# A fused cross-attention and quantised feed-forward kernel: the weights and late inputs are loaded and prepared later

## What is computed

```python
qk = einsum('bhdq,bhdl->bhql', qh, kh) * scale
ret = einsum('bhql,bhdl->bhdq', softmax(qk), vh)      # values = keys = ctx
x = x + gamma * ret
# bit_linear: einsum(activation_quant(x), weight_quant(w))
h = silu(bit_linear(xn, w_gate)) * bit_linear(xn, w_up)   # xn = layernorm(x); w: 1024 x 256
x = x + bit_linear(rms_norm(h, ln_weight), w_down)        # w_down: 256 x 1024
```

## Time and profile before

| | us |
|---|---|
| median of 3 runs | 229.3 |
| the profiled execution, its own time | 227.79 |
| its span in the trace | 226.0 |
| busy in the span: PE / VectorE / ScalarE / GpSimd | 169.6 / 148.8 / 135.3 / 115.8 |

### The profile page before, as it was taken

One profiled execution on the slowest core, in us unless ns is written; L12 is line 12 of the kernel. 1 busy time (PEld: TensorE's weight loads), 2 busy tenths in 40 slices (PEclk: granted clock), 3 DMA queues, 4 the chain that ended last, 5 costly groups with the idle time before them and its releaser, 6 DMA issues.

```text
span 226.0 us, 4319 instructions
## 1 busy us (share of the span) xinstructions
PE 169.6 (75%) x1382; PEld 97.5 (43%) x1382; DVE 148.8 (66%) x284; ACT 135.3 (60%) x274; POOL 115.8 (51%) x290
## 2 busy tenths in 40 slices
PE   0005561787798969898998989889989988973792
PEld 0002530553375533555465556455655644522332
DVE  2304662536465964897997899799899895246283
ACT  3124252653337754868868886886876975971432
POOL 4327435330523173676786587587367448347150
PEclk9999985558569985999999999999999997997589
DMA  5765989318502162026306315422600000000000
GB/s 160 235 135 156 325 214 244 97 20 179 117 0 74 48 151 64 23 70 144 98 17 174 84 40 128 99 83 79 149 11 5 0 28 7 0 23 0 26 0 23
DMA packets 15707, 19.95 MB, mean 88 GB/s; under 512 B 2597, under 2 KB 14005, under 8 KB 14677
## 3 DMA queue, kind: packets, MB, share of 16 engines
q1 hardware_dynamic: 11397, 14.43, 25.6%
q10 hardware_dynamic: 4288, 5.24, 8.3%
HBM read 15.20 MB, written 4.19 MB: 86 GB/s over the span
## 4 chain that ended last, share of the span: by engine, by line
PE 34%; POOL 25%; DVE 12%; issue 11%; DMA 9%; ACT 6%; ACTq 2%; POOLq 0%; DVEq 0%
PE psO L465 7%; PE psA L435 6%; PE psB L449 5%; POOL hw L317 5%; DMA q_stack<-mt 3%; PE psG L538 3%; POOL hq L1020 3%; DMA k_stack<-k_scratch 3%; DVE h L855 2%; DVE mneg L763 2%; DVE gu L844 2%; ACT th L679 2%; PE psG L501 2%; PE psU L501 2%; PE psG L575 2%
## 5 line engine op out<-in xcount | busy, mean ns | idle before, releaser
L763 DVE TENSOR_REDUCE mneg<-psA 128x2 f32<-128x512 f32 x128 | 82.2, 678 | 26.8 <-PE psA L435 26.6
L608 ACT ACTIVATE probs<-psB 128x512 f32<-128x512 f32 x128 | 73.5, 596 | 26.2 <-PE psB L449 25.4
L435 PE MATMUL psA<-k_stack,q_stack 72*128 72x256 bf16 x256 | 53.8, 299 | 19.7 <-DMA k_stack<-k_scratch 19.3
L449 PE MATMUL psB<-q_stack,k_stack 75*128 75x256 bf16 x256 | 51.9, 288 | 6.6 <-DMA q_stack<-mt 4.6
L465 PE MATMUL psO<-probs,vt 128*32 128x256 f32 x512 | 37.7, 416 | 1.0 <-ACT probs L608 1.0
L435 PEld LDWEIGHTS psA<-k_stack,q_stack 72*128 72x128 bf16 x256 | 23.1, 105 | 34.7 <-issue 27.9
L449 PEld LDWEIGHTS psB<-q_stack,k_stack 75*128 75x128 bf16 x256 | 23.5, 102 | 20.9 <-DMA q_stack<-mt 5.4
L317 POOL TENSOR_TENSOR hw<-h,lnw 128x512 f32<-128x512 f32 x15 | 19.2, 1278 | 22.3 <-DVE h L855 13.3
L465 PEld LDWEIGHTS psO<-probs,vt 128*32 128x32 f32 x512 | 14.1, 115 | 15.2 <-issue 8.8
L844 DVE SCALAR_TENSOR_TENSOR gu<-th,psG 128x512 f32<-128x512 f32 x15 | 10.3, 688 | 9.9 <-ACT th L679 9.9
L679 ACT ACTIVATE th<-psG,tscale 128x512 f32<-128x512 f32 x15 | 10.3, 688 | 8.5 <-PE psG L538 8.5
(11 more groups left out here) (134 smaller groups left out, 256.3 us busy)
## 6 DMA issues: line engine op xcount, KB each, us to landing
k_stack<-k_scratch SPq DMA_DIRECT2D x21, 192.0 KB
q_stack<-q_scratch SPq DMA_DIRECT2D x21, 192.0 KB
q_scratch<-q_parts SPq DMA_DIRECT2D x24, 64.0 KB, 2.6
k_scratch<-k_parts SPq DMA_DIRECT2D x21, 64.0 KB, 2.1
w_sb<-in_L_ffn_w_gate_dram ACTq DMA_DIRECT2D x1, 1024.0 KB, 6.0
w_sb<-in_L_ffn_w_up_dram ACTq DMA_DIRECT2D x1, 1024.0 KB, 6.0
w_sb<-in_L_ffn_w_down_dram ACTq DMA_DIRECT2D x1, 1024.0 KB, 15.6
out_dram<-y_sb SPq DMA_DIRECT2D x8, 128.0 KB, 1.9
```

Source lines behind the costliest of these rows:

```text
L435: mm = pe.matmul(psA[n % A_BANKS][:, qt * L:(qt + 1) * L], q_stack[0:STACK, t % NBUF, bh, qt * P:(qt + 1) * P], k_stack[0:STACK, t % NBUF, ...
L449: mm = pe.matmul(psB[b % 2][:, lt * L:(lt + 1) * L], k_stack[:, t % NBUF, bh, lt * P:(lt + 1) * P], q_stack[:, t % NBUF, bh, :], start=Tru ...
L608: act.activation(probs[:, b % RING, :], psB[b % 2][:, :], ACT.Exp, scale=SCALE).then_inc(s_exp, 1)
L763: dve.tensor_reduce(mneg[:, k % MBUF, QT * (bh % HALF):QT * (bh % HALF + 1)], psA[n % A_BANKS][:, :].rearrange("p (q l) -> p q l", q=QT), ...
```

## The change

The gate's load leaves the start of ScalarE's queue, up and down leave its step -4, and the late inputs leave its step 19. All are now issued by SyncE behind a transfer of maxima: tile 3's inputs and the gate behind the second (steps 36, 37), tile 4's inputs and up and down behind the third (52, 53), the inputs of tiles 5 to 7 at step 85. The stack load of tile 1 moves from step 5 to step 21, behind the first transfer of maxima and, within step 21, behind the stores of tile 2, which stand at that step already. The preparation of the gate moves from steps -8 to 17 to steps 38 to 56, that of up from 22 to 40 to 66 to 81, that of down from 34 to 52 to 78 to 97. Six instead of four groups are copied by VectorE. The variances of tiles 3 to 7 are taken in three lots. Waits in the feed-forward part are refined to the weights that are needed.

```diff
-ACT_W, ACT_LATE = -4, 19
-EARLY = 3
+EARLY, FIRST_LOAD = 3, 21
+BULK_W = {37: (0,), 53: (1, 2)}
+BULK_XC = {36: (3, 4), 52: (4, 5), 85: (5, 8)}
...
-ACT_WS, PE_W, DVE_W, POOL_WQ, DVE_WQ = (-8, 22, 34), (3, 26, 38), (3, 26, 38), (4, 27, 39), (8, 32, 44)
-WB = {10: 0, 12: 1, 14: 2, 17: 3, 34: 4, 36: 5, 38: 6, 40: 7, 46: 8, 48: 9, 50: 10, 52: 11}
-WB_ON_DVE = (5, 7, 9, 11)
-POOL_INIT, DVE_STATS = 46, 45
+ACT_WS, PE_W, DVE_W, POOL_WQ, DVE_WQ = (38, 66, 78), (42, 69, 84), (42, 69, 84), (43, 70, 88), (48, 75, 92)
+WB = {50: 0, 52: 1, 54: 2, 56: 3, 76: 4, 78: 5, 80: 6, 81: 7, 94: 8, 95: 9, 96: 10, 97: 11}
+WB_ON_DVE = (1, 3, 5, 7, 9, 11)
+STATS = {-32: (1, 3), 45: (3, 4), 77: (4, 5), 109: (5, 8)}
...
+        def load_xc(eng, a, b):
+            for t in range(a, b):
+                eng.dma_start(x_sb[:, t, :], x_rows[t]).then_inc(s_x[t], DMA)
+                eng.dma_start(c_sb[:, t, :], ctx_rows[t]).then_inc(s_c[t], DMA)
...
+                if m in BULK_W:
+                    for k in BULK_W[m]:
+                        load_w(sp, k)
+                if m in BULK_XC:
+                    load_xc(sp, *BULK_XC[m])
                 t = tile_at(m, SP_STORE)
...
-                t = tile_at(m, SP_LOAD)
+                t = 1 if m == FIRST_LOAD else tile_at(m, SP_LOAD) if m > FIRST_LOAD else None
...
-                            pe.wait_ge(s_wT, 12 - len(WB_ON_DVE))
-                            pe.wait_ge(s_wTd, len(WB_ON_DVE))
+                            for k in (6, 7):
+                                pe.wait_ge(*w_copied(k))
...
-            load_w(act, 0)
...
-                if m == ACT_W:
-                    act.wait_ge(s_first, 2 * PARTS * DMA)
-                    act.wait_ge(s_stack[0], 2 * PARTS * DMA)
-                    load_w(act, 1)
-                    load_w(act, 2)
-                if m == ACT_LATE:
-                    act.dma_start(x_sb[:, EARLY:T, :], x_rows[EARLY:T].rearrange("g p l -> p g l")).then_inc(s_x[EARLY], DMA)
-                    act.dma_start(c_sb[:, EARLY:T, :], ctx_rows[EARLY:T].rearrange("g p l -> p g l")).then_inc(s_c[EARLY], DMA)
```

More of the change, by code:

```diff
@@ L195, in build @@
         banks = (psG, psU)
-        s_x = [sem(f"x_loaded{i}") for i in range(EARLY + 1)]
-        s_c = [sem(f"ctx_loaded{i}") for i in range(EARLY + 1)]
+        s_x = [sem(f"x_loaded{i}") for i in range(T)]
+        s_c = [sem(f"ctx_loaded{i}") for i in range(T)]
         s_w = [sem(f"w_loaded{i}") for i in range(3)]
@@ L472, in _ @@
                     take(BANK_CTX, s_vt, 2 * (t + 1))
-                    pe.wait_ge(s_c[min(t, EARLY)], DMA)
+                    pe.wait_ge(s_c[t], DMA)
                     for lt in range(LT):
@@ L569, in _ @@
                     take(BANK_DOWN, s_out, u + 1)
+                    for k in (10, 11):
+                        if u == 0:
+                            pe.wait_ge(*w_copied(k))
                     for ic in range(IC):
@@ L621, in _ @@
                         act.wait_ge(s_qst[t % 2], PARTS * DMA * (t // 2))
-                    act.wait_ge(s_c[min(t, EARLY)], DMA)
+                    act.wait_ge(s_c[t], DMA)
                     act.activation(k_parts[:, t % 2, 0, :], c_sb[:, t, :], ACT.Copy).then_inc(s_p1, 1)
@@ L746, in _ @@
                 n, after = divmod(m, 2)
-                if m in (2 * FIRST, DVE_STATS):
-                    tiles = range(1, EARLY) if m == 2 * FIRST else range(EARLY, T)
-                    for t in range(tiles[0], min(tiles[-1], EARLY) + 1):
+                if m in STATS:
+                    tiles = range(*STATS[m])
+                    for t in tiles:
                         dve.wait_ge(s_x[t], DMA)
@@ L947, in _ @@
                             pool.memset(vt[:, b, :, :, i, 2 * DH * i + DH:2 * DH * i + DH + 1], 1.0).then_inc(s_vt0, 1)
-                if m == POOL_INIT:
-                    pool.wait_ge(s_xvar, 3)
-                    rstd_of(EARLY, T)
+                if m - 1 in STATS and m > 0:
+                    a, b = STATS[m - 1]
+                    pool.wait_ge(s_xvar, 2 + list(STATS).index(m - 1))
+                    rstd_of(a, b)
                 if m in POOL_WQ:
@@ L978, in _ @@
                         else:
-                            pool.wait_ge(s_wm, 3)
+                            pool.wait_ge(s_wm, 2)
                         pool.tensor_tensor(a_sig[:, :], a_inv[:, :], minus_one[:, 0:1], ALU.pow).then_inc(s_asig, 1)
@@ L1015, in _ @@
                     pool.tensor_tensor(h_sig[:, :], h_rec[:, :], cr[:, :], ALU.mult).then_inc(s_hsig, 1)
+                    if u == 0:
+                        pool.wait_ge(s_wm, 3)
                     pool.tensor_tensor(yscale[:, :], h_inv[:, :], wmean[:, 2:3], ALU.mult).then_inc(s_ysc, 1)
```

## The result

The changed kernel takes 241.2 us (median of 4 runs, 238.8 to 245.15) beside 229.7 for the kernel before; the ratio is 1.053 with a 95% interval of 1.034 to 1.073. It is slower, as forecast, and by more than forecast (236.0). The profiled execution has 238.8 us and a span of 237.0, against 227.79 and 226.0. All 11 us of difference are there at step 128; behind it both kernels take 113.7 to 113.8 us.

A forecast was written before the change was run, and what follows sets the result against it. It took VectorE as starved for pass A's scores, with a slow key store and first maxima transfer in the early chain. Terms -1.0 at step 64, +7, +1 made 7 us later: 234.8 profiled, 236.0 forecast, range 224 to 242.

The forecast's parts named there:

- Steps 1 and 2: Kernel start: no gate load beside tile 0's stores, pass A at 16.9 (2.4 us gained); pass B 27.6, gain 13.
- Step 3: Tile 1's six late stack loads take 9.9 us; tile 1 starts at 39.0, leaving 2.8 of 13 us gain.
- the short end: Tile 1's stack loads landing like the 128 KB loads, 4.2 us earlier; the skill's fit puts tile 1 at 35.
- Step 4: Tile 1: ScalarE's sum waits for the late gate load; kernel steps 42, 43 reached at 52.0, gain down to 1.2 us.
- Step 5: Kernel steps 43 to 64: same work, no better clock, 0.2 us lost; tile 2 begins at 70.8, 1.0 earlier.
- Step 6: Tile 2, kernel steps 64 to 96: added weight work, mainly its order, costs 7 us; bounds 0 and 11.
- The gross 11.2: Tile 2: listed waits for sums and up's limiting plus added transpose groups, 11.2 us before deductions.
- the 4.2 taken off: Tile 2 deductions: wait of 2.0 us for ScalarE's copy, then covered, and some 2.2 lost at half clock.
- Step 7: Tile 3, kernel steps 96 to 128: two more groups and three tiles' variances cost 1 us; bounds 0 and 3.
- Rival A: Faster: early gain survives at kernel steps 32 and 38, tile 2 at the engines' floor; 222 us, chance 0.18.
- Rival B: No change: weight work fills tile 2's idle time, order costs only the floor; 232 us, chance 0.30.

The follow-up runs named there:

- The gate early again: Changed kernel with the gate's load issued by ScalarE at the very start, as before the change: 239.0 us, ratio 1.045 to the kernel before.
- The stacks early again: Changed kernel with tile 1's stack load issued at step 5 again, ahead of the first transfer of maxima: 234.3 us, ratio 1.025 to the kernel before.

## Why the prediction was right

Direction and mechanism hold; the size (+7 forecast, +11 in the profile) is off in three terms, steps 5, 6 and 7. Tile 2 and tile 3 both lie beyond the bounds that were given for them, and step 5 erred the other way, so it is in part luck that the time lies in the range.

- **Steps 1 and 2, start and first transfer:** right. Pass A at 15.65 (16.9), pass B at 25.41 (27.6); the gain at the start was 3.6, just beyond its bound of 3.5. The gate early again takes just this back.
- **Step 3, tile 1's stacks:** right, 39.06 (39.0), but the exact hit is luck: tile 0 began 1.25 us sooner and the loads took 11.3 us instead of 9.9. The ten microseconds of a stack load, taken from tile 4's rows, held here, not the short end. The stacks early again show it from the other side: 5.3 us sooner, and a transfer wait of 7.4 instead. By the fit of the Trainium skill ("DMA: Bandwidth & Descriptors", "Anatomy of one DMA") this start would have been at 35; the measurement disagrees.
- **Step 4, the gate's load:** right, 52.68 (52.0), with ScalarE waiting 7.18 us and TensorE 5.80 behind it. The gate early again took 6.3 us out of steps 32 to 43 and left the stack wait.
- **Step 5, the rest of tile 1:** missed. "I take no better clock" was wrong: 13.8 us instead of 18.6, at full pace from 57 on, so tile 2 began 5.35 us early, not 1.0. The step took the work to be "the same kind and amount", but the variances on VectorE had fallen from five tiles (2.2 us) to one (0.6). The prediction had named 3 us for the better clock and put it into the rival, and had named a clock of 1.00 from step 43 on as a sign of being wrong. This sign came: the window from 52.68 to 66.47 reads 1.00.
- **Step 6, tile 2:** right in kind, mis-sized, +11.6 for +7 with an upper bound of 11. The gross 11.2 was near; the 4.2 taken off was the failed term. The wait of 2.0 us for ScalarE's copy shrank to 0.81 only, beside a new one of 0.57 for a copy of VectorE's, and the lost clock was not won back: 0.82 against 0.84. Of the listed waits, the sum at step 66 came at 2.12 (2.0) and up's limiting at 1.93 (3.5). The 2.72 us for down's limiting at step 94 had no term. The idle time grew by 6.1 us and the busy time by 5.4, where six groups had been put at 5.2; but cutting most of those matmuls gave nothing, so that agreement is not a confirmation.
- **Step 7, tile 3:** mis-sized, +4.9 for +1 with an upper bound of 3. The variance lot of tiles 5 to 7 was costed by its length on VectorE (1.5 us), not by who waits behind it: GpSimd's power, its normalised tile, ScalarE's copy, and TensorE for 2.68 us. Moving the lot took that wait away and 1.9 us of the tile. The other 3.0 us are not split up; the clock of 0.90, where the kernel before had 1.00, is in them.
- **Sum:** against the forecast, step 64 came 4.3 us sooner (66.47 for 70.8), tile 2 took 4.6 us more (33.2 for 28.6), tile 3 3.9 more (23.7 for 19.8): some 4.1 us in all, step 128 at 123.3 for 119.2.

Rival A failed at its first condition, tile 1 before 35. Rival B failed in tile 2: the weights did not fill idle time. Late preparation by itself costs 2.5% with all loads as before; with the stacks early again the changed kernel stands at 1.025 instead of 1.053. So late preparation alone makes about half of the loss, and putting one load back takes about half of it away; the intervals are too wide for a finer split.

**What stays open.** Why the granted clock falls when it does. In the changed kernel a window after 12 us of idling reads 1.00, dummy work ahead of tile 1 did not hold the pace, and less TensorE work came with a lower clock. So the busy growth of 5.4 us in tile 2 cannot be split into work and clock, and no run here gives tile 2 the late preparation at 1.00 (it had 0.70 to 0.85). Whether another shape of the stack loads would land sooner was not tested either.

## What to carry to other kernels

Moving a load behind an urgent transfer pays only while its user has other work before it: here the 15 us won at the start went into the stack load that had been put behind it (12.2 us) and into the gate's sum (5.8 us), which stands one step behind its load's issue. Beware of long preparation in a stage that is close to full: price every piece by what is queued behind it on each engine, down to the last user, not by its own busy time. Before moving megabytes, look for one batched piece ahead of a short chain; splitting one lot of variances gave 2.4%, moving loads alone 1.6%, with intervals that overlap.

## What the runs showed of the hardware

- PEclk is not the pace in all stretches, so paces (start to start) are to be read from the rows. In the window 39.06 to 52.68 of the changed kernel it reads 1.00, and yet the pairs of the two passes follow each other every 0.43 us, twice the 0.22 us of later. Timeline of TensorE in the changed kernel:

```profile
39.88 0.63 PE L447 MATMUL psA<-k_stack,q_stack 72*128 72x256 bf16 x2
40.31 0.63 PE L461 MATMUL psB<-q_stack,k_stack 75*128 75x256 bf16 x2
...
57.26 0.38 PE L461 MATMUL psB<-q_stack,k_stack 75*128 75x256 bf16 x2
57.48 0.38 PE L447 MATMUL psA<-k_stack,q_stack 72*128 72x256 bf16 x2
```

- Six stack loads of 192 KB took 11.3 us from first issue to use with no weights or inputs beside them (27.79 to 39.06).
- Six stack loads issued ahead of a 12 KB transfer moved pass B from 25.41 to 32.53. With weights and inputs beside it too, a transfer issued at 28.45 held pass B until 43.43.
- Fewer matmuls did not mean less busy time: with 17 fewer in tile 2 the granted clock was 0.73 instead of 0.82 and TensorE was busy 0.6 us longer. This is one profile each; whether the one brought the other is not shown.
